# Channel attention with four tiles weighed at once, scores issued together, and fillers at the openings of the stages

## What is computed

```python
x = x + tanh(g_xattn[0]) * L0_xattn(layernorm(x), ctx, ...)   # self and cross attention, 16 heads of 128, fp8 rounding
x = x + tanh(g_ffn[0])   * L0_ffn(layernorm(x), ...)          # router, 8 of 32 experts
x = x + tanh(g_xattn[1]) * L1_xattn(layernorm(x), ctx, ctx, gamma)
x = x + tanh(g_ffn[1])   * L1_ffn(layernorm(x), ...)          # MLP with four-bit weights

def L1_xattn(q, k, v, gamma):        # channel attention: attends between the 256 columns
    # (batch, 64, 256) -> (batch, 8 heads, 8 channels, 256)
    qk = einsum('bhdq,bhdl->bhql', qh, kh) / sqrt(8)
    return gamma * einsum('bhql,bhdl->bhdq', softmax(qk), vh)
```

## Time and profile before

| | us |
|---|---|
| runs | 1055.1, 1056.71, 1056.92 |
| profiled execution, its own time | 1055.09 |
| its span, first to last instruction | 1053.3 |
| TensorE matmul busy | 921.4 (87%) |
| VectorE busy | 752.2 (71%) |
| ScalarE busy | 564.0 (54%) |
| GpSimd busy | 277.6 (26%) |
| mean granted clock of TensorE | 0.955 |

### The profile page before, as it was taken

How to read it: one execution, slowest core, us unless ns; L and a number is a source line. 1 busy time by engine, 2 the same in 40 slices (tenths; PEclk the granted TensorE clock), 3 DMA queues, 4 the chain that set the end, 5 groups by cost and what they waited for, 6 DMA issues and landing times. The chain is left out here.

```text
span 1053.3 us, 19229 instructions
## 1 busy us (share of the span) xinstructions
PE 921.4 (87%) x6928; PEld 758.8 (72%) x6928; DVE 752.2 (71%) x1235; ACT 564.0 (54%) x1713; POOL 277.6 (26%) x412
## 2 busy tenths in 40 slices
PE   1579999989999999647999999987999997799997
PEld 1578888888888889546777777764666664577776
DVE  7778898898989897665444444455788888657553
ACT  6677878787877877314333333232555554333332
POOL 1133333333333344012322222201101112223230
PEclk9989999999999999876999999995999997899999
DMA  3101010110101000023111110010000000110001
GB/s 143 41 1 61 2 62 10 53 59 4 61 1 62 2 22 1 1 95 132 48 49 48 49 48 3 0 37 24 1 1 0 0 0 7 54 61 30 30 0 40
DMA packets 10776, 35.35 MB, mean 34 GB/s; under 512 B 1232, under 2 KB 5328, under 8 KB 8400
## 3 DMA queue, kind: packets, MB, share of 16 engines
q1 hardware_dynamic: 10560, 34.38, 9.1%
q10 hardware_dynamic: 144, 0.03, 0.0%
HBM read 33.36 MB, written 1.05 MB: 33 GB/s over the span
## 5 line engine op out<-in xcount | busy, mean ns | idle before, releaser
L216 PE MATMUL ps<-wt_hi,xq 128*128 128x256 f32 (+1 forms) x512 | 124.2, 279 | 20.1 <-DVE ctx_lo L719 14.5
L216 PE MATMUL ps<-wt_lo,xq 128*128 128x256 f32 (+1 forms) x512 | 123.7, 283 | 0.0
L216 PEld LDWEIGHTS ps<-wt_hi,xq 128*128 128x128 f32 x512 | 99.9, 195 | 22.9 <-DVE ctx_lo L719 14.9
L362 ACT ACTIVATE square<-ps 128x128 bf16<-128x128 f32 x384 | 100.6, 294 | 26.7 <-PE ps L216 26.6
L1524 ACT ACTIVATE ca_probs<-ps 128x512 f32<-128x512 f32 x128 | 69.5, 595 | 82.9 <-PE ps L1444 82.9
L216 PEld LDWEIGHTS ps<-wt_lo,xq 128*128 128x128 f32 x512 | 99.7, 195 | 0.0
L1584 DVE TENSOR_REDUCE context_mx<-ps 128x4 f32<-128x1024 f32 x64 | 76.9, 1201 | 26.3 <-PE ps L1416 26.3
L1110 POOL TENSOR_TENSOR moe_w_lo<-moe_w_all,moe_w_hi 128x384 fp32r<-128x384 f32 x48 | 55.3, 1187 | 135.0 <-ACT moe_w_hi L1211 135.0
L509 POOL TENSOR_TENSOR rstd<-rstd,half_neg 128x6 f32<-128x6 f32 x64 | 88.2, 1378 | 5.0
L362 ACT ACTIVATION_READ_ACCUMULATOR square<-ps 128x1 f32 x384 | 85.9, 226 | 0.0
L1275 DVE TENSOR_TENSOR moe_act_g<-moe_act_g,ps 128x512 f32<-128x512 f32 x48 | 33.1, 689 | 72.1 <-PE ps L1146 72.1
(11 more groups left out here) (215 smaller groups left out, 2593.0 us busy)
## 6 DMA issues: line engine op xcount, KB each, us to landing
moe_w_all<-in_experts SPq DMA_DIRECT2D x8, 1152.0 KB, 5.2
w_in<-in_wt SPq DMA_DIRECT2D x8, 1024.0 KB, 5.9
wp_in<-in_wp SPq DMA_DIRECT2D x8, 512.0 KB, 3.7
ffn_codes<-in_codes SPq DMA_DIRECT2D x8, 384.0 KB, 3.2
ffn_w_scales<-in_code_scales SPq DMA_DIRECT2D x8, 384.0 KB, 3.7
x_rows<-in_x SPq DMA_DIRECT2D x2, 512.0 KB, 4.6
ctx_in<-in_ctxT SPq DMA_DIRECT2D x1, 1024.0 KB, 8.9
context_rows<-in_ctx SPq DMA_DIRECT2D x1, 1024.0 KB, 10.8
```

Of the source, the lines that this page charges most:

```text
L216: last = mm(ps[:, first + bank, col:col + width], left[:, c, tokens], w[:, c, wcol:wcol + width], start=(j == 0), stop=(j == len(steps) - 1))
L362: last = nc.scalar.activation(square[:, i % 2, j, :], ps[:, bank, (j % 4) * P:(j % 4) * P + P], ACT.Square, scale=float(HD) ** -0.5, accum ...
```

## The change

- **`weigh`** is called twice a batch instead of four times, with four heads each, in the four quarters (32 columns each) of the array's columns. `vmask` has 32 columns a head: 16 for values (two heads of a quarter's turn share them), and two for sums. `probs` has eight tiles, one a head. The output lies in bank 7.
- **VectorE** then transposes the bank in blocks of 32 x 32 (`turn_values`), takes 16 reciprocals a partition (`invert`), multiplies two halves with them (`scale_values`), and every second batch transposes back (`turn_back`) and adds 128 x 256 to `x`.
- **`row_scores`** issues the two heads of a pair in turn, and has two pairs of banks (0/1 and 2/3), shared with `turn_maxima`. **`column_scores`** and `replicate` share the three banks 4, 5 and 6 in turn; `column_scores` waits until the use before the last one is taken. `qk_rows` has three sets, `mT` two.
- **`replicate`** has two matmuls: `split` holds a batch's high parts on partitions 0 to 63 and its low parts on 64 to 127. `split_high` and `split_low` fill it, for the context in the stage before, for `h` in this one (two tiles first, six later).
- The context turned comes by a DMA of 1 MB in the stage before; the transposes and copies at the opening go. `spread` has 4 matrices instead of 16.
- All loops over batches are written out.
- **Fillers** (`keep_busy`: float32 matmuls of the identity with 512 columns, their output not used): three at the end of the first stage, five at the opening of the second and three before the router's turn, five and two at the opening of channel attention, two and two at the opening of the last stage.

```diff
+def keep_busy(nc, k, bank, count):
+    for _ in range(count):
+        nc.tensor.matmul(k.ps[:, bank, :].rearrange("p (r n) -> p r n", r=4), k.ident[:],
+                         k.ident[:].unsqueeze(1).broadcast_to([P, 4, P]), start=True, stop=True)
...
+            keep_busy(nc, k, 2, 3)
...
+            if self.interleaved and j == CH:
+                keep_busy(nc, k, 7, 2)
...
+def split_high(copy, split, rows, first, last, done):
+    for par in range(2):
+        dst = split[0:64].rearrange("p (n b) f -> p n b f", b=2)[:, first:last, par]
+        copy(dst, rows[64 * par:64 * par + 64, first:last]).then_inc(done, 1)
+def split_low(nc, split, rows, first, last, done):
+    for par in range(2):
+        pairs = split[:].rearrange("p (n b) f -> p n b f", b=2)[:, first:last, par]
+        low = nc.vector.tensor_tensor(pairs[64:128], rows[64 * par:64 * par + 64, first:last], pairs[0:64].bitcast(F32), ALU.subtract)
...
+            keep_busy(nc, k, G_BANK, 5 if moe else 2)
...
+                        keep_busy(nc, k, R_BANK, 3)
...
+                for which, src in enumerate((split, c_split)):
+                    last = mm(ps[:, B_BANK + n % 3, which * HID:which * HID + HID], spread[:, 2 * group + which, :], src[:, b, :],
+                              start=True, stop=True)
...
+                for qt in range(CH):
+                    for e in range(2):
+                        group, rows = cut(2 * pair + e)
+                        last = mm(ps[:, A_BANK + 2 * (n % 2) + e, qt * HID:qt * HID + HID], qk_rows[rows, b % 3, group, 0, qt * P:qt * P + P],
+                                  qk_rows[rows, b % 3, group, 1, :], start=True, stop=True)
...
-            def weigh(i, par, pair, first=False):
-
-                pe.wait_ge(s["exp_done"], C_HEADS * (2 * i + par) + 2 * pair + 2)
...
-                for c in range(CH):
-                    for e in range(2):
-                        last = mm(ps[64 * e:64 * e + 64, OUT_BANK[par], 0:HID], vmask[:, par, c, pair + 4 * e, :],
...
+            def column_scores(b, pair):
+                n = b_use["head", b, 2 * pair]
+                if pair == 0:
+
+                    pe.wait_ge(s["a_taken"], a_use(b, TURN) + 1)
+
+                pe.wait_ge(s["b_taken"], n - 1)
...
+            def weigh(b, turn):
+                pe.wait_ge(s["b_taken"], b_use["head", b, 4 * turn + 3] + 1)
...
+                for c in range(CH):
+                    for quarter in range(4):
+                        t, e = divmod(quarter, 2)
+                        last = mm(ps[32 * quarter:32 * quarter + 32, OUT_BANK, 0:HID], vmask[:, b % 2, c, 2 * turn + t + 4 * e, :],
+                                  probs[:, 4 * turn + quarter, c * HID:c * HID + HID],
+                                  start=(turn == 0 and c == 0), stop=(turn == 1 and c == CH - 1))
+                last.then_inc(s["pv_done"], 1)
+
+            keep_busy(nc, k, OUT_BANK, 5)
+            pe.wait_ge(s["h_low"], 2)
+            replicate(0, 0)
+            replicate(0, 1)
+            row_scores(0, 0)
...
+            for b in range(BATCH):
+                if b + 2 < BATCH:
+                    replicate(b + 2, 0)
+                if b + 1 < BATCH:
+                    row_scores(b + 1, 1)
+                column_scores(b, 0)
+                if b + 1 < BATCH:
+                    row_scores(b + 1, 2)
+                column_scores(b, 1)
+                if b > 0:
+                    weigh(b - 1, 1)
+                if b + 1 < BATCH:
+                    row_scores(b + 1, 3)
+                column_scores(b, 2)
+                if b + 2 < BATCH:
+                    replicate(b + 2, 1)
+                weigh(b, 0)
+                if b + 1 < BATCH:
+                    turn_maxima(b + 1)
+                if b + 2 < BATCH:
+                    row_scores(b + 2, 0)
+                column_scores(b, 3)
+            weigh(BATCH - 1, 1)
...
+            def turn_values(b):
+                dve.wait_ge(s["pv_done"], 2 * (b + 1))
+                nc.vector.transpose(turned[:], ps[:, OUT_BANK, 0:HID]).then_inc(s["out_taken"], 1)
+
+            def invert(b):
+                dve.wait_ge(s["out_taken"], b + 1)
+                nc.vector.reciprocal(inv[:], turned[:].rearrange("p (b r) -> p b r", r=32)[:, :, 2 * C_DIM:2 * C_DIM + 2]
+                                     ).then_inc(s["inverted"], 1)
...
+            for b in range(BATCH):
+                if b == 1:
+                    dve.wait_ge(s["rest_high"], 2)
+                    split_low(nc, split, h, FIRST_TILES, TILES, s["rest_low"])
+                if b + 1 < BATCH:
+                    maxima(b + 1, 1)
+                    maxima(b + 1, 2)
+                if b == BATCH - 1:
+                    k.ffn.vector_stats_ahead(dve, s["weighed"])
+                if b > 0:
+                    turn_values(b - 1)
+                if b + 1 < BATCH:
+                    maxima(b + 1, 3)
+                if b > 0:
+                    invert(b - 1)
+                    scale_values(b - 1)
+                if b > 0 and b % 2 == 0:
+                    turn_back(b // 2 - 1)
+                if b + 1 < BATCH:
+                    take_maxima(b + 1)
+                if b > 0 and b % 2 == 0:
+                    add_values(b // 2 - 1)
+                if b + 2 < BATCH:
+                    maxima(b + 2, 0)
```

More of the change, by code:

```diff
@@ L817, in sync @@
         sp.dma_start(self.minus_in[:], a["minus"]).then_inc(self.minus_arrived, 16)
+        sp.dma_start(self.turned[:], a["ctxT"]).then_inc(self.turned_in, 16)
     def scalar(self, act):
         act.wait_ge(self.rows_in, 16)
[L821 removed]
+        split_high(self.nc.scalar.copy, self.split, self.rows, 0, TILES, self.high)
     def scalar_constants(self, act):
@@ new lines, in turn_maxima @@
+            def turn_maxima(b):
+                n = a_use(b, TURN)
+                pe.wait_ge(s["a_taken"], n)
+                for qt in range(CH):
+                    last = nc.tensor.transpose(ps[:, A_BANK + 2 * (n % 2), qt * P:qt * P + P], mx[:, qt, :], ident[:])
+                last.then_inc(s["a_ready"], 1)
+            def column_scores(b, pair):
[3 more added lines that the diff above has]
+                pe.wait_ge(s["b_taken"], n - 1)
@@ L1465, in batch @@
-            def batch(i, par, first=False, scores_after=True, rows_after=True):
-                ni, npar = (i, 1) if par == 0 else (i + 1, 0)
-                for pair in range(C_HEADS // 2):
-                    if scores_after:
-                        row_scores(ni, npar, pair)
-                    column_scores(i, par, pair, first)
-                    if pair == 0 and scores_after:
-                        replicate(ni, npar, 1)
-                    if pair == 2 and rows_after:
-                        if first:
-                            pe.wait_ge(s["h_low"], 2)
-                        replicate(i + 1, par, 0)
-                    if pair >= 1:
-                        weigh(i, par, pair - 1, first)
-                if scores_after:
-                    turn_maxima(ni, npar)
-                weigh(i, par, C_HEADS // 2 - 1, first)
@@ L1486, in _ @@
-            for j in range(2 * CH):
-                half, c = divmod(j, CH)
-                for t in range(4):
-                    last = nc.tensor.transpose(ps[:, j, t * P:t * P + P], c_rows[:, half * 4 + t, c * P:c * P + P], ident[:])
-                last.then_inc(s["c_turned"], 1)
-            pe.wait_ge(s["h_low"], 1)
-            replicate(0, 0, 0, first=True)
-            replicate(0, 0, 1)
-            pe.wait_ge(s["c_copied"], 2 * CH)
-            for pair in range(4):
-                row_scores(0, 0, pair, first=(pair == 0))
-                if pair == 0:
-                    replicate(0, 1, 0)
@@ new lines, in _ @@
+            keep_busy(nc, k, OUT_BANK, 5)
[3 more added lines that the diff above has]
+            row_scores(0, 0)
+            replicate(1, 0)
+            row_scores(0, 1)
+            replicate(1, 1)
+            for pair in range(2, PAIRS):
+                row_scores(0, pair)
+                keep_busy(nc, k, OUT_BANK, 1)
+            turn_maxima(0)
+            row_scores(1, 0)
+            for b in range(BATCH):
[20 more added lines that the diff above has]
+                column_scores(b, 3)
@@ L1597, in take_values @@
-            def take_values(i, par):
-                b = 2 * i + par
-                dve.wait_ge(s["inverted"], CH * (b + 1))
-                for half in range(2):
-                    rows, sums = [slice(at, at + C_ROWS) for at in (64 * half, 64 * half + C_ROWS)]
-                    to = slice(64 * par + C_ROWS * half, 64 * par + C_ROWS * half + C_ROWS)
-                    last = nc.vector.scalar_tensor_tensor(part[to, :], ps[rows, OUT_BANK[par], 0:HID], gain[rows, 0:1], inv[sums, :],
-                                                          ALU.mult, ALU.mult)
-                last.then_inc(s["out_taken"], 1)
```

348 lines of the change are left out of this document (153 added, 195 removed).

## The result

| us | before | after |
|---|---|---|
| median of 8 runs (lowest, highest) | 1056.03 (1054.76, 1057.38) | 1051.35 (1041.18, 1058.82) |
| profiled execution, its span | 1055.09, 1053.3 | 1057.21, 1055.4 |
| mean granted clock | 0.955 | 0.921 |

The ratio is 0.9914 with an interval of 0.9897 to 0.9932; this ratio and those of the experiments leave out a kernel's slow runs, over 1.5% above its fastest (here three of eight), while the medians have all runs and give 0.9956 here. The forecast was 1019, the range 1004 to 1037: the measurement lies outside. Runs of the new kernel spread over 18 us, those of the old one over 3.

The account below looks back on a forecast made before the run. TensorE's queue was taken as the bound, 9.3 us of a 9.83 us batch. Terms -30 - 5.1 - 0.7 - 2.9 + 3.0 - 0.7 = -36.4 us, from 1055.09, gave 1018.7, forecast as 1019, range 1004 to 1037.

Parts of the forecast that it names:

- the fifteen periods: Channel attention's steady batches: each falls from 9.83 to 7.8 us (bounds 6.9 and 8.3), gaining 30 us (23 to 44).
- The clock falls in the stage: Rival, chance 0.07: TensorE's pauses in channel attention drop the clock, making the kernel slower; 1070 at three quarters low.
- 1.3 us of pauses a batch, in several pieces, leave TensorE 83% occupied: Argument against the low-clock rival in channel attention: TensorE has 6.5 us of work in a 7.8 us period.
- The rival's arithmetic: Low-clock batches in channel attention: TensorE's sum some 11.5, period 12.3 us; about 1053 with half the stage low.
- the rival of 1041: Channel attention's weighing: four matmuls do not run abreast, a turn takes 1.9 us, the period about 9.3; chance 0.12.
- the rival of 1036: VectorE in channel attention: transposes or strided access are dear, 1.2 us each, adding 1.2 a batch; chance 0.12.
- the sum of three loops: Steady period: TensorE 6.5, ScalarE 6.6 and VectorE 6.9 us hang on each other; with 0.9 added, 7.8.
- The opening with the clock up: Channel attention's opening: first copied maxima at 721.6, a gain of 5.1 us, with five fillers holding the clock.
- The stage before: Before channel attention: splitting the context delays the router's choice 4.1 us, fillers give back 1.1; sum +3.0.
- The end: Channel attention's last copied maxima to its finish, 16.0 us before: GpSimd ends at +13.1, gain 2.9 us (0 to 5).
- The last stage's opening: Two and two fillers fit TensorE's idle 6.5 us: -0.7 us (-1.5 to +3.4, both at the low level).
- The opening's fillers: Five at channel attention's opening hold the clock, ending by 711.4 or 715.6: cost taken 0 (bounds 0 and +1.4).

Follow-up runs that it names:

- eight_only: Changed kernel with eight fillers instead of five at channel attention's opening and none in the batches: 1046.6 us, ratio 0.991.
- eight_first: Changed kernel with two fillers a batch, ahead of column scores of pairs 0 and 1, and eight fillers for five at channel attention's opening: 1026.0 us, 0.971.
- weigh_twice: eight_only with every weighing turn issued twice, the first copy into unused columns: 1074.2 us, ratio 1.017.
- twice_filled: weigh_twice plus two fillers a batch, ahead of the column scores of pairs 0 and 1: 1049.1 us, ratio 0.995.
- fillers_behind: eight_first with its two batch fillers moved behind the first weighing turn and behind the last column scores: 1032.4 us, ratio 0.979.
- weigh_earlier: eight_only with the last batch's second weighing turn issued ahead of the column scores of pair 1, not behind: 1035.8 us (1027.1 to 1041.4), 0.983.
- earlier_best: best with the second weighing turn ahead of pair 1's column scores and only one batch filler, ahead of pair 0: 1027.9 us (1019.8 to 1051.6), 0.969.
- best: eight_first with the context's split moved into the steps of the stage before, as in context_later: 1019.5 us, ratio 0.964.
- context_later: two_fillers with the context's split moved out of the way of the router's choice in the second stage: 1023.7 us (1017.5 to 1029.9), ratio 0.971.
- four_fillers: Changed kernel with four fillers a batch, two ahead of pair 0 and one each ahead of pairs 1 and 3: 1060.4 us, ratio 0.999.
- two_fillers: Changed kernel with two fillers a batch, ahead of the column scores of pairs 0 and 1: 1025.3 us, ratio 0.970.
- fp32r_all: two_fillers with the fillers in the batches and at channel attention's opening as fp32r matmuls instead of float32: 1042.0 us (1027.1 to 1048.9), 0.979.
- one_steady: eight_first with only one filler a batch, ahead of pair 0: 1033.5 us, ratio 0.978.

## Why the prediction was wrong

**The failed step** is that the fifteen periods were taken at a clock of 1.00 (7.8 us each), with the rival to it at 0.07. "The clock falls in the stage" came true: granted 0.66 over 125 us, where the text asked for 1.00 from 715 on and named anything under 0.95 as wrong. The step that ruled it out was "1.3 us of pauses a batch, in several pieces, leave TensorE 83% occupied". The pauses were there, fewer than forecast (two, 0.8 us marked idle a batch), and the clock fell all the same. The cause is tested twice: two fillers a batch in these pauses, and nothing else changed, take the clock from 0.80 to 1.00 and the time from 1046.6 to 1026.0 (eight_only, eight_first), and from 0.76 to 1.00 and from 1074.2 to 1049.1 (weigh_twice, twice_filled). The Trainium skill ("TensorE: Matmul & The Clock Gate", "A second HAM failure mode"), cited there beside the rival, says that short idles between groups alone can make the clock swing; these two pairs of runs agree (0.76 in weigh_twice, 1.00 in twice_filled), and fillers_behind, weigh_earlier and earlier_best, which kept 1.00 with a pause or two left, show that such idles need not do it. I set the rival aside because the clock was 1.00 in mid-stage before, where TensorE had its own short waits. It had one, of 0.19 us, a batch, against two of 0.4; the windows from 775 to 850, before and after:

```profile
801.18 0.51 PE L1416 MATMUL ps<-ca_qk_rows 32*128 32x256 f32 x4 [0.19 <-DVE context_mx L1584]
```

```profile
775.00:850.00 75.00, 73.63 (x628) 47.45 (x626) 61.42 (x77) 39.90 (x76) 9.38 (x64) 1.00 0.00 0
```

```profile
775.00:850.00 75.00, 70.94 (x602) 41.02 (x602) 51.86 (x78) 39.74 (x75) 9.27 (x64) 0.69 0.00 1
```

The rival's arithmetic came out close, in part by luck. It counts batches: 1053 with half of them low, 1070 with three quarters. A mean of 0.66 is the low level for 0.68 of the time, which at 7.8 and 12.3 us a batch is 0.57 of the batches, so 1057, and the profiled run took 1057.2 (the median is 1051.4). (Its TensorE sum of "some 11.5" is 11.7 by its own 6.5 and 1.8.) But the fifteen periods were 30.0 us over the forecast and not the 38.5 that this gives (low ones took up to 11.8 us, and most batches were low in part only), and the other stretches were 8.5 us over it.

**What held.** Four abreast: 1.00 us forecast as 1.01, so the rival of 1041 did not come. Transposes, reciprocal and multiplication within 50 ns each, so the rival of 1036 did not come either. The period at full clock: 7.80 in weigh_earlier, which has no fillers in its batches, forecast 7.8; in best, 7.9 with two. That the sum of three loops and an allowance of 0.9 for their hanging together came out exact is luck in part: TensorE's sum was 6.6 (7.9 less two fillers of 0.63), forecast 6.5, but `row_scores` take 0.33 to 0.44 us a pair, not 0.24. The opening with the clock up: in best the first maxima come 14.2 us after the stage's start (707.84 to 722.06), forecast 14.5 (707.1 to 721.6). With the clock held, eight_first is at 1026.0, fillers included, and its fifteen periods take 121.0 us for 150.4: 29.4 of the forecast's 30.7 us are in the kernel, and the clock hides them.

**Terms mis-sized besides.** In eight_first's profiled run (1026.53, 7.8 us over the sum's 1018.7) the five stretches of the table are +5.4, -4.9, -29.4, -1.5 and +2.0, so the periods and the opening are 1.6 us over the forecast and the first, fourth and fifth 6.5. The first three terms below are given as the kernel after has them:
- *The stage before*, +5.0 for +3.0. The router's turn came 4.5 later (forecast 4.1), and the -1.1 from the fillers beside it did not come. (The turn is at 497.22 against 492.73; with the split moved it is at 489.88 in context_later and at 493.1 in best.)
- *The end*, -1.5 for -2.9. GpSimd was late next, as said, but started at 889.24, 10.9 us after the last maxima, not 9.1: VectorE's unpacking began only after the values of batch 14 had waited 1.38 us for their weighing. (The prediction's own terms, 7.6 + 1.47 + 3.85, come to 12.9 and not the 13.1 that it has.)
- *The last stage's opening*, +1.9 for -0.7. The first two fillers ran at the low level (four instructions marked 3.75) and held the transposes behind them for 3.6 us; the next two ran mostly at the high level (2.11 marked, 898.97) but stand ahead of the second half of the transposes, which starts 7.2 us after the stage's start, before the change 4.5. This is inside the -1.5 to +3.4 that the text gave, on the bad side.
- *The opening's fillers*, of which the prediction prices only the first five: the single ones behind `row_scores` of pairs 2 and 3 stand ahead of the scores and the transposes that VectorE waits for, and at the low level are marked some 2.08 us each (723.33), at the high one 1.12 in best.

## What to carry to other kernels

A change that takes work off the bounding engine opens pauses on it, and TensorE's granted clock is then a term of the sum with a chance of its own, not a remark: price the period at both levels before trusting a gain of 20%. Read the clock by windows within the stage and compare runs, since a spread of 18 us where there was 3 is itself a sign of it. Fill a pause at its own place, ahead of the wait (1026.0, against 1032.4 with the fillers elsewhere), with just its length of work; filling beyond the pause is paid in full (four_fillers). Useful work moved into a pause costs nothing (weigh_earlier), but by itself it did not make the runs steady.

## What the runs showed of the hardware

- TensorE stayed at 0.50 to 0.56 for some 50 us (720 to 770) in two_fillers, with no pause marked from 740 on (30.00 busy of 30 from 740 to 770), and then rose to 1.00 with the work unchanged and stayed; four_fillers and fp32r_all did the same until 780. A full queue did not bring the clock back quickly here, while eight_only, with pauses, went from 0.50 to 0.78 and 0.90 in the next windows.
- Added work made the kernel faster twice: two_fillers against the kernel after by 26 us, twice_filled against weigh_twice by 25 us.
- Four float32 matmuls on 32 columns each take as long as two on 64: 16 instructions in 1.00 us against 8 in 1.01. The order in which the quarters are issued does not matter (1.02). One turn at the low level takes 1.87.
- A transpose of 128x256 float32 in blocks of 32 x 32 took VectorE 449 ns from PSUM and 446 ns from SBUF, against 418 for its copy of 128x256 in the same stretch.
- **Open:** why weigh_earlier kept the clock with two pauses a batch in its traced run, and why one_steady (one pause of 0.42 to 0.44 us a batch, at 800.27, 808.06 and 817.31) loses it now and then while fillers_behind, with one as long at the same place, held it for 100 us. One_steady has one filler a batch less than fillers_behind, and its pauses come in turn 7.8 and 9.2 us apart, not 8.0; between these two runs the amount of work and the spacing are not separated. That filling the two pauses, ahead of the column scores of pairs 0 and 1, keeps the clock is shown; the rule behind it is not.
